# Graph attention in fp32 on one core: the reciprocals of the softmax sums are turned as 32 columns and spread by DMA instead of as 128 columns copied out by ScalarE

## Chip, cores, metric

One core of one Trainium2 chip runs the whole program in one launch. The metric is the device time in microseconds; each kernel is run several times, and the median counts. The host only transposes and permutes arrays before the launch.

## What is computed

32 graphs of 256 nodes and 256 features, 8 heads of 32 features. Cut to what matters:

```python
q, k, v = proj(x, Wq, bq), proj(x, Wk, bk), proj(x, Wv, bv)      # 8 heads of 32
scores  = einsum('bhqd,bhkd->bhqk', q, k) * 32 ** -0.5
attn    = softmax(scores * (adj + adj), axis=-1)
ctx     = einsum('bhqk,bhkd->bhqd', attn, v)
out     = layernorm(x + ctx.reshape(b, 256, 256) @ Wo.T + bo)
```

The kernel works with unnormalised exponentials: it sums each row of `exp(...)`, and multiplies the context by the reciprocal of that sum. The change is about how these reciprocals ("shares": 256 nodes x 8 heads for a graph) get to the layout of the context.

## The kernel before, in words

Engines: TensorE (PE), VectorE (DVE), ScalarE (ACT), GpSimd (POOL), SyncE (SP, which only issues DMAs). Every engine runs its own stream of instructions, in an order that is written out by hand as a loop of steps: `step(g)` for graph g, with eight slots `o` = 0 to 7, one for each head. Waits on semaphores tie the streams together. An instruction never overtakes the one before it on its engine.

Slot o of step g holds, on each engine, among other things:

- **PE**: `turn_probs(g, o)` (four transposes of 128x128, the exponentials of head o, L263), then `rows` (two matmuls, the scores of the head four ahead, L251); further, by slot: at o = 1 `weigh_v(g-1)` (the context of the graph before, 32 matmuls into `ctx_bank`, L337), at o = 2 `turn_shares(g-1)` (L313), at o = 4 `project_v(g+2)` (L307), at o = 7 `project_out(g-1)` (L351), and at o = 0 or 3, 5 and 6 a half of `project_kq` (three matmuls of 512 columns into the one `proj_bank`, L291). The half at o = 5 is the first of a new chunk and waits until ACT has read the chunk before out of `proj_bank` (`kq_out`, L287).
- **DVE**: `reduce_rows` (scores times mask with a running maximum, L415) for the head three ahead, `move_turned(g, o)` (`turn_bank` to SBUF, L430; for o = 0 and 4 ACT does it), `lower_top` (L423); at o = 0 to 3 residual and statistics, at o = 4 `scale_context(g-1)` (L443), at o = 6 `divide(g)` (the reciprocals, L436).
- **ACT**: `exp` (two activations, L542) for the head two ahead, `move_turned` for o = 0 and 4 (L552), at o = 4 (and 7) `read_kq` (`proj_bank` to SBUF, L573), at o = 3 `copy_inverse(g-1)` (L558). In the stream the last of these stands right behind `exp(g, 5)`, and `exp(g, 6)`, `move_turned(g, 4)` and `read_kq` follow it.
- **POOL**: cuts values into a high and a low fp32r part, bias, normalisation, and at o = 7 `spread_shares(g)` (L681).
- **SP**: `fill_stacks` fills the stacks of K and Q of a pair of graphs with 16 DMAs of 256 KB (two per `fill`, L187): eight for K once `cut_kq` number 1 is through, eight for Q once number 3 is; and a load of x. SP works only in odd steps.

The path of the shares before: DVE makes them as 128 partitions x 16 (`shares`); POOL copies each 32 times side by side (`wide`, 128x512); PE turns `wide` with four 128x128 transposes into `inv_bank`; ACT copies `inv_bank` (128x512) to `inverse`; DVE multiplies the context by `inverse`.

```python
319                wait(pe, inverted, g)
320                for half_ in range(2):
321                    for t in range(T):
322                        last = nc.tensor.transpose(inv_bank[:, half_ * S + t * P:half_ * S + (t + 1) * P],
323                                                   wide[:, t, J * half_:J * (half_ + 1), :].rearrange("p h d -> p (h d)"),
324                                                   ident[:])
```

Of the kernel before, what the change touches and what calls it, by code (L numbers as in the profile page):

```python
# [18 lines left out]
P = 128  # L19
B, S, E = 32, 256, 256  # L20
H, D = 8, 32
T = S // P
J = P // D
# [2 lines left out]
LOWEST = -3.4028234e38  # L26
FACTOR = 2.0 * float(D) ** -0.5
RING = 4
TURNED = 12


# [10 lines left out]
def build(nc, x, x_t, adj, adj_t, wq, wk, wv, wo, bq, bk, bv, bo, out):  # L42
    ctx = ExitStack()
    with ctx:
        def sb(name, shape, dt=F32):
            return ctx.enter_context(nc.sbuf_tensor(name, shape, dt))
# [4 lines left out]
        def sem(name):  # L51
            return ctx.enter_context(nc.semaphore(name))
# [13 lines left out]
        top = sb("top", [P, 2, H, T])  # L66
        low_top = sb("low_top", [P, 2, H, T])
        sums = sb("sums", [P, 2, T, H])
        shares = sb("shares", [P, T, H])
        probs = sb("probs", [P, RING, T * S])  # L70
        turned_probs = sb("turned_probs", [P, TURNED, T * S])
        wide = sb("wide", [P, T, H, D])
        inverse = sb("inverse", [P, 2 * S])
        context = sb("context", [P, 2 * S])
        ctx_parts = sb("ctx_parts", [P, 2, 2, 2, S], F32R)
# [5 lines left out]
        ident = sb("ident", [P, P])  # L81
# [26 lines left out]
        rows_made, rows_used, top_ready = sem("rows_made"), sem("rows_used"), sem("top_ready")  # L108
        probs_ready, turned = sem("probs_ready"), sem("turned")
        moved_dve, moved_act = sem("moved_dve"), sem("moved_act")  # L110
        shares_ready, widened, inv_made = sem("shares_ready"), sem("widened"), sem("inv_made")
        ctx_made, inverted, ctx_ready = sem("ctx_made"), sem("inverted"), sem("ctx_ready")
        ctx_high, ctx_low = sem("ctx_high"), sem("ctx_low")
        out_made, y_ready, stats_ready, mean_ready = (
# [9 lines left out]
        def wait(eng, what, value):  # L124

            if value > 0:
                eng.wait_ge(what, value)
# [22 lines left out]
        def is_graph(g):  # L150
            return 0 <= g < B

        def is_pair(g):
            return 0 <= g // 2 < PAIRS
# [37 lines left out]
        @block.sync  # L192
        def _(sp):
            for t in range(T):
                sp.dma_start(xt[:, t, :], x_t[0][:, t * 2 * S:(t + 1) * 2 * S]).then_inc(xt_first[t], 16)
            sp.dma_start(w_whole[:, 1], wq).then_inc(weight_in[1], 16)
            for tile, bias_dram in ((b_k, bk), (b_q, bq)):
                sp.dma_start(tile[:], bias_dram.rearrange("(j d) t -> d j t", j=J)).then_inc(biases_in, 16)
            for n, dram in ((2, wv), (3, wo)):
                sp.dma_start(w_whole[:, n], dram).then_inc(weight_in[n], 16)  # L200
            for tile, dram in ((b_v, bv), (b_o, bo)):
                sp.dma_start(tile[:], dram).then_inc(biases_in, 16)

            def load_x_t(pair):

                sp.wait_ge(xt_low, 2 * pair)
                sp.dma_start(xt[:].rearrange("p t s -> p (t s)"), x_t[pair]).then_inc(xt_in, 16)

            def fill_stacks(pair):
                for which in range(2):  # L210
                    sp.wait_ge(kq_low, 4 * pair + 2 * which + 2)
                    for j in range(J):
                        if pair > 1:

                            sp.wait_ge(rows_made, 8 * (2 * pair - 3) + 2 * j + 2)
                        fill(sp, pair, which, j)

            def step(g):
                if g % 2 == 0:
                    return  # L220
                if is_pair(g + 5):
                    load_x_t((g + 5) // 2)
                if is_pair(g + 3):
                    fill_stacks((g + 3) // 2)

            load_x_t(1)
            for j in range(J):
                fill(sp, 0, 0, j)
            load_x_t(2)

            sp.wait_ge(kq_low, 4)
            for j in range(J // 2, J):
                fill(sp, 0, 1, j)
            fill_stacks(1)
            run_steps(step)

        @block.tensor
        def _(pe):
# [72 lines left out]
                last.then_inc(v_made, 1)  # L311

            def turn_shares(g):  # L313
                pe.wait_ge(widened, g + 1)
                if g == 0:

                    pe.wait_ge(bias_ready, 1)

                wait(pe, inverted, g)
                for half_ in range(2):  # L320
                    for t in range(T):
                        last = nc.tensor.transpose(inv_bank[:, half_ * S + t * P:half_ * S + (t + 1) * P],  # L322
                                                   wide[:, t, J * half_:J * (half_ + 1), :].rearrange("p h d -> p (h d)"),
                                                   ident[:])
                last.then_inc(inv_made, 1)

            def weigh_v(g):
                pe.wait_ge(v_ready, g + 1)
# [52 lines left out]
            def step(g):  # L381
                for o in range(H):
                    if is_graph(g):
                        turn_probs(g, o)
                    if o < 4 and is_graph(g):
                        rows(g, o + 4)
                    if o >= 4 and is_graph(g + 1):
                        rows(g + 1, o - 4)
                    if (g % 2, o) in KQ_SLOTS:
                        ahead = kq_ahead(g, o)  # L390
                        if is_pair(g + ahead):
                            project_kq((g + ahead) // 2, *KQ_SLOTS[g % 2, o])
                    if o == 1 and g == 0:
                        project_v(1)
                    if o == 1 and is_graph(g - 1):
                        weigh_v(g - 1)
                    if o == 2 and is_graph(g - 1):
                        turn_shares(g - 1)
                    if o == 4 and is_graph(g + 2):
                        project_v(g + 2)  # L400
                    if o == 7 and is_graph(g - 1):
                        project_out(g - 1)

            run_steps(step)

        @block.vector
        def _(dve):
# [24 lines left out]
            def divide(g):  # L432
                dve.wait_ge(probs_ready, H * g + H)

                wait(dve, widened, g)
                nc.vector.reciprocal(shares[:], sums[:, g % 2]).then_inc(shares_ready, 1)  # L436

            def scale_context(g):
                dve.wait_ge(ctx_made, g + 1)
                dve.wait_ge(inverted, g + 1)  # L440

                wait(dve, ctx_low, g)
                nc.vector.tensor_tensor(context[:], ctx_bank[:], inverse[:], ALU.mult).then_inc(ctx_ready, 1)  # L443
# [84 lines left out]
        def _(act):  # L528
# [22 lines left out]
                    act.wait_ge(bias_ready, 1)  # L551
                nc.scalar.copy(turned_probs[:, (H * g + o) % TURNED, :], turn_bank[o % 2][:]).then_inc(moved_act, 1)  # L552

            def copy_inverse(g):
                act.wait_ge(inv_made, g + 1)

                wait(act, ctx_ready, g)
                nc.scalar.copy(inverse[:], inv_bank[:]).then_inc(inverted, 1)  # L558

            def cut_x(pair, t):  # L560
                if pair == 0:
# [64 lines left out]
            def step(g):  # L626
                for o in range(H):
                    if o < 6 and is_graph(g):
                        exp(g, o + 2)
                    if o >= 6 and is_graph(g + 1):  # L630
                        exp(g + 1, o - 6)
                    if is_graph(g) and o in ON_ACT:
                        move_turned(g, o)
                    if o == 1 and g % 2 == 0 and is_pair(g + 2):
                        load_masks((g + 2) // 2)
                    if o == 2 and g % 2 == 0 and is_pair(g):
                        load_x(g // 2)
                    if (g % 2, o) in KQ_CUT_SLOTS:
                        ahead = kq_ahead(g, o)
                        if is_pair(g + ahead):  # L640
                            read_kq((g + ahead) // 2, KQ_CUT_SLOTS[g % 2, o])
                    if o == 2 and g == 0:
                        copy_v(1)
                    if o == 3 and is_graph(g - 1):
                        copy_inverse(g - 1)
                    if o == 5 and is_graph(g + 2):
                        copy_v(g + 2)
                    if (g % 2, o) in X_SLOTS and is_pair(g + 4):
                        cut_x((g + 4) // 2, X_SLOTS[g % 2, o])
                    if o == 2 and is_graph(g - 3):  # L650
                        store(g - 3)
# [6 lines left out]
        def _(pool):  # L658
# [13 lines left out]
            def low_x(pair, t):  # L672
                pool.wait_ge(xt_high, 2 * pair + t + 1)
                nc.gpsimd.tensor_tensor(xt_parts[:, pair % 2, 1, t, :], xt[:, t, :], xt_parts[:, pair % 2, 0, t, :].bitcast(F32),  # L674
                                        ALU.subtract).then_inc(xt_low, 1)

            def spread_shares(g):
                pool.wait_ge(shares_ready, g + 1)

                wait(pool, inv_made, g)  # L680
                nc.gpsimd.tensor_copy(wide[:].rearrange("p t h d -> p (t h) d"),  # L681
                                      shares[:].rearrange("p t h -> p (t h)").unsqueeze(2).to_broadcast([P, T * H, D])
                                      ).then_inc(widened, 1)

            def cut_context(g):
                high, low = (ctx_parts[:, g % 2, n].rearrange("p f s -> p (f s)") for n in range(2))
# [47 lines left out]

            def step(g):
                for o in range(H):
                    if o == 7 and is_graph(g):
                        spread_shares(g)
                    if (g % 2, o) in X_SLOTS and is_pair(g + 4):
                        low_x((g + 4) // 2, X_SLOTS[g % 2, o])  # L740
                    if o == 2 and is_graph(g - 1):
# [56 lines left out]
```

## Time and profile before

| | |
|---|---|
| median of 3 runs | 473.74 us (472.96 to 474.92) |
| the profiled execution, its own time | 472.42 us |
| its span, first to last instruction | 470.6 us |
| busy: PE, DVE, ACT, POOL | 446.9, 403.4, 384.3, 345.4 us |
| granted PE clock, mean | 0.988 of full speed |

The sums further on are made against the profiled execution. Busy times of an engine are overlapped with those of the others. A matmul's duration in the timeline reaches from its start to its modelled end, and matmuls overlap, so what a group of matmuls occupies of PE is read from its start to the start of the next group.

### The profile page before, as it was taken

The numbers are of one execution on the slowest core, as the hardware profiler recorded it, in microseconds if no ns is written. First come the engines' busy times: TensorE is split into PE (matmuls) and PEld (weight loads), VectorE is DVE, ScalarE is ACT, GpSimd is POOL, SyncE is SP. The second block draws the span as 40 slices with busy tenths as digits, with TensorE's granted clock in tenths as the row PEclk, the third lists the DMA queues.
The fourth block names the chain that finished last, engine by engine and source line by source line (L and its number), as shares of the span: only waits on it lengthen the run. The fifth ranks groups of instructions, "written<-read, shape, count | busy, mean of one in ns | idle before, by whom it ended". The sixth has DMA issues, their size and how long they took to land.

```text
span 470.6 us, 13017 instructions
## 1 busy us (share of the span) xinstructions
PE 446.9 (95%) x3846; PEld 380.7 (81%) x3846; DVE 403.4 (86%) x1712; ACT 384.3 (82%) x1252; POOL 345.4 (73%) x476
## 2 busy tenths in 40 slices
PE   5889999999999999999999999999999999999962
PEld 4588888988888898888888888888888888888642
DVE  4568889998888898988889988888998888899961
ACT  5488889888888988888899888889988888888840
POOL 0464787869698786968878696878869687865555
PEclk9999999999999999999999999999999999999995
DMA  6986655658666564867656476765647685462211
GB/s 223 353 312 231 242 214 169 251 184 288 247 236 255 169 253 172 286 247 258 234 180 255 183 262 248 272 239 179 252 181 247 247 287 206 158 256 93 70 36 45
DMA packets 37319, 102.57 MB, mean 218 GB/s; under 512 B 5889, under 2 KB 14082, under 8 KB 37250
## 3 DMA queue, kind: packets, MB, share of 16 engines
q1 hardware_dynamic: 23474, 75.26, 43.5%
q10 hardware_dynamic: 13776, 26.48, 16.6%
q8 instruction: 32, 0.52, 0.4%
q14 instruction: 37, 0.30, 0.2%
HBM read 26.22 MB, written 8.39 MB: 74 GB/s over the span
## 4 chain that ended last, share of the span: by engine, by line
PE 84%; DVE 7%; issue 4%; ACT 3%; POOL 2%; DMA 1%; POOLq 0%; DVEq 0%; ACTq 0%
PE turn_bank L263 21%; PE proj_bank L291 18%; PE ctx_bank L337 11%; PE row_bank L251 11%; PE out_bank L351 9%; PE out_bank L307 9%; DVE probs L415 4%; PE inv_bank L322 3%; ACT probs L542 2%; PE row_bank L276 1%; DMA turned_probs<-in_wk 1%; DVE low_top L423 1%; POOL xt_parts L674 1%; DVE stats L455 1%; PE turn_bank L276 1%
## 5 line engine op out<-in xcount | busy, mean ns | idle before, releaser
L542 ACT ACTIVATE probs<-probs,low_top 128x256 f32<-128x256 f32 x512 | 255.7, 503 | 55.9 <-DVE low_top L423 51.8
L415 DVE CUSTOM_DVE_ANT_0 probs<-row_bank,adj_rows 128x256 f32<-128x256 f32 x512 | 192.0, 413 | 7.7 <-PE row_bank L251 5.5
L430 DVE COPY turned_probs<-turn_bank 128x512 f32<-128x512 f32 x192 | 132.3, 689 | 36.7 <-PE turn_bank L263 35.6
L263 PE MATMUL turn_bank<-ident,probs 128*128 128x128 f32 x1024 | 155.3, 274 | 3.1 <-ACT turned_probs L552 1.4
L263 PEld LDWEIGHTS turn_bank<-ident,probs 128*128 128x128 f32 x1024 | 120.9, 140 | 32.8 <-ACT probs L542 16.5
L251 PE MATMUL row_bank<-stack 128*128 128x256 f32 x512 | 123.2, 322 | 2.6 <-issue 1.7
L291 PE MATMUL proj_bank<-xt_parts,w_parts 128*128 128x512 f32 x360 | 105.2, 401 | 1.8 <-ACT whole L573 1.3
L542 ACT ACTIVATION_READ_ACCUMULATOR probs<-probs,low_top 128x1 f32 x512 | 97.7, 191 | 0.0
L251 PEld LDWEIGHTS row_bank<-stack 128*128 128x128 f32 x512 | 77.1, 191 | 5.2 <-issue 4.2
L668 POOL TENSOR_TENSOR parts<-whole,parts 128x512 fp32r<-128x512 f32 x60 | 77.3, 1288 | 5.0
L689 POOL CAST ctx_parts<-context 128x512 fp32r<-128x512 f32 x32 | 19.6, 612 | 73.7 <-DVE context L443 73.7
L291 PEld LDWEIGHTS proj_bank<-xt_parts,w_parts 128*128 128x128 f32 x360 | 59.2, 188 | 11.2 <-issue 1.5
L337 PE MATMUL ctx_bank<-turned_probs,v 128*32 128x256 f32 x1024 | 61.9, 382 | 0.0
L351 PE MATMUL out_bank<-w_parts,ctx_parts 128*128 128x256 f32 x384 | 52.0, 286 | 3.9 <-POOL ctx_parts L691 3.9
L351 PEld LDWEIGHTS out_bank<-w_parts,ctx_parts 128*128 128x128 f32 x384 | 48.7, 193 | 4.4 <-POOL ctx_parts L691 4.4
L307 PE MATMUL out_bank<-w_parts,xt_parts 128*128 128x256 f32 x384 | 51.2, 283 | 0.0
L674 POOL TENSOR_TENSOR xt_parts<-xt,xt_parts 128x512 fp32r<-128x512 f32 x30 | 38.6, 1305 | 15.3 <-ACT xt_parts L567 15.3
L307 PEld LDWEIGHTS out_bank<-w_parts,xt_parts 128*128 128x128 f32 x384 | 48.1, 191 | 0.4 <-issue 0.4
L337 PEld LDWEIGHTS ctx_bank<-turned_probs,v 128*32 128x32 f32 x1024 | 30.0, 109 | 20.9
L691 POOL TENSOR_TENSOR ctx_parts<-context,ctx_parts 128x512 fp32r<-128x512 f32 x32 | 41.3, 1292 | 2.6
L666 POOL CAST parts<-whole 128x512 fp32r<-128x512 f32 x60 | 37.0, 617 | 8.5 <-DMA stack<-parts 5.5
L415 DVE DVE_READ_ACCUMULATOR2_ANT top<- 128x1 f32 x512 | 42.8, 83 | 0.0
(48 smaller groups left out, 462.1 us busy)
## 6 DMA issues: line engine op xcount, KB each, us to landing
stack<-parts SPq DMA_DIRECT2D x252, 256.0 KB, 3.2
adj_rows<-in_adj ACTq DMA_DIRECT2D x16, 512.0 KB, 4.5
xr<-in_x ACTq DMA_DIRECT2D x16, 512.0 KB, 7.2
out<-result ACTq DMA_DIRECT2D x32, 256.0 KB, 4.7
xt<-in_x_t SPq DMA_DIRECT2D x15, 512.0 KB, 5.0
stack<-parts ACTq DMA_DIRECT2D x4, 256.0 KB, 3.8
xt<-in_x_t SPq DMA_DIRECT2D x2, 256.0 KB, 3.6
turned_probs<-in_wk ACTq DMA_DIRECT2D x1, 256.0 KB, 3.7
```

What stands on the lines that cost most here:

```text
L251: last = nc.tensor.matmul(row_bank[o % 2][:, t * S:(t + 1) * S], q[:, t * P:(t + 1) * P], key, start=(t == 0), stop=True, skip_group_check ...
L263: last = nc.tensor.transpose(turn_bank[o % 2][:, c * S + t * P:c * S + (t + 1) * P], probs[:, o % RING, t * S + c * P:t * S + (c + 1) * P] ...
L291: last = nc.tensor.matmul(proj_bank[:], w_parts[:, a, c // 2, t, features], xt_parts[:, pair % 2, b, t, :], start=(half_ == 0 and n == 0), ...
L307: last = nc.tensor.matmul(out_bank[:, tile * E:(tile + 1) * E], xt_parts[:, (n // 2) % 2, a, t, nodes], w_parts[:, c, 2, t, :], start=(til ...
L337: last = nc.tensor.matmul(ctx_bank[c:c + D, half_ * S:(half_ + 1) * S], v[:, (g // 2) % 2, g % 2, t, o * D:(o + 1) * D], turned_probs[:, ( ...
L351: last = nc.tensor.matmul(out_bank[:, n * E:(n + 1) * E], ctx_parts[:, g % 2, a, f, nodes], w_parts[:, b, 3, f, :], start=(n == 0 and i == 0),
L415: last = nc.vector.tensor_tensor_reduce(probs[:, o % RING, t * S:(t + 1) * S], row_bank[o % 2][:, t * S:(t + 1) * S], adj_rows[:, (n // 2) ...
L430: nc.vector.tensor_copy(turned_probs[:, (H * g + o) % TURNED, :], turn_bank[o % 2][:]).then_inc(moved_dve, 1)
L542: last = nc.scalar.activation(tile, tile, ACT.Exp, bias=low_top[:, n % 2, o, t:t + 1], accum_out=sums[:, n % 2, t, o:o + 1])
L668: nc.gpsimd.tensor_tensor(parts[:, 2 * (c // 2) + 1, cut], whole[:, c % 2, :], parts[:, 2 * (c // 2), cut].bitcast(F32), ALU.subtract).the ...
L674: nc.gpsimd.tensor_tensor(xt_parts[:, pair % 2, 1, t, :], xt[:, t, :], xt_parts[:, pair % 2, 0, t, :].bitcast(F32), ALU.subtract).then_inc ...
L691: nc.gpsimd.tensor_tensor(low, context[:], high.bitcast(F32), ALU.subtract).then_inc(ctx_low, 1)
```

## The change

The shares are now made four times side by side (128x64). PE turns 32 columns a tile: two transposes whose stationary side is 128x32 and whose moving side is the 128-column identity, at o = 7 of the same step, behind `project_out`. ACT copies 32 partitions x 256 columns to `share_rows` at o = 0 of the next step. SP then issues two DMAs; each reads 16 partitions of `share_rows` and writes every row to eight partitions of `inverse`. POOL's copy is gone. DVE's multiplication waits for both DMAs. SP's fills for a pair stand in another order: the K fills of a pair, and six of its Q fills, in an even step behind the spread of the shares; the last two Q fills and the load of x in the odd step, behind the spread there.

```diff
-        shares = sb("shares", [P, T, H])
+        shares = sb("shares", [P, T, H * SPREAD])
-        wide = sb("wide", [P, T, H, D])
+        share_rows = sb("share_rows", [H * SPREAD, T * P])
...
+            def spread_shares(g):
+                sp.wait_ge(rows_out, g + 1)
+
+                wait(sp, ctx_ready, g)
+                for half_ in range(2):
+                    rows = J * SPREAD
+                    sp.dma_start(inverse[:, half_ * S:(half_ + 1) * S],
+                                 share_rows[rows * half_:rows * (half_ + 1), :].unsqueeze(1).to_broadcast(
+                                     [rows, D // SPREAD, S])).then_inc(inverted, 16)
 
             def step(g):
+                if is_graph(g - 1):
+                    spread_shares(g - 1)
                 if g % 2 == 0:
-                    return
-                if is_pair(g + 5):
-                    load_x_t((g + 5) // 2)
-                if is_pair(g + 3):
-                    fill_stacks((g + 3) // 2)
+                    if g > 0 and is_pair(g + 2):
+                        fill_stack((g + 2) // 2, 0, range(J))
+                    if is_pair(g + 2):
+                        fill_stack((g + 2) // 2, 1, range(J - 1))
+                else:
+                    if is_pair(g + 1):
+                        fill_stack((g + 1) // 2, 1, [J - 1])
+                    if is_pair(g + 5):
+                        load_x_t((g + 5) // 2)
...
             def turn_shares(g):
-                pe.wait_ge(widened, g + 1)
+                pe.wait_ge(shares_ready, g + 1)
...
-                wait(pe, inverted, g)
-                for half_ in range(2):
-                    for t in range(T):
-                        last = nc.tensor.transpose(inv_bank[:, half_ * S + t * P:half_ * S + (t + 1) * P],
-                                                   wide[:, t, J * half_:J * (half_ + 1), :].rearrange("p h d -> p (h d)"),
-                                                   ident[:])
-                last.then_inc(inv_made, 1)
+                wait(pe, rows_out, g)
+                for t in range(T):
+                    last = nc.tensor.transpose(inv_bank[0:H * SPREAD, t * P:(t + 1) * P], shares[:, t, :], ident[:])
+                last.then_inc(shares_turned, 1)
...
-                    if o == 2 and is_graph(g - 1):
-                        turn_shares(g - 1)
...
+                    if o == 7 and is_graph(g):
+                        turn_shares(g)
...
-                wait(dve, widened, g)
-                nc.vector.reciprocal(shares[:], sums[:, g % 2]).then_inc(shares_ready, 1)
+                wait(dve, shares_turned, g)
+                nc.vector.reciprocal(shares[:].rearrange("p t (h r) -> p (t h) r", r=SPREAD),
+                                     sums[:, g % 2].rearrange("p t h -> p (t h)").unsqueeze(2).to_broadcast(
+                                         [P, T * H, SPREAD])).then_inc(shares_ready, 1)
...
-                dve.wait_ge(inverted, g + 1)
+                dve.wait_ge(inverted, 32 * g + 32)
...
-            def copy_inverse(g):
-                act.wait_ge(inv_made, g + 1)
-
-                wait(act, ctx_ready, g)
-                nc.scalar.copy(inverse[:], inv_bank[:]).then_inc(inverted, 1)
+            def copy_shares(g):
+                act.wait_ge(shares_turned, g + 1)
+
+                wait(act, inverted, 32 * g)
+                nc.scalar.copy(share_rows[:], inv_bank[0:H * SPREAD, 0:T * P]).then_inc(rows_out, 1)
...
+                    if o == 0 and is_graph(g - 1):
+                        copy_shares(g - 1)
...
-                    if o == 3 and is_graph(g - 1):
-                        copy_inverse(g - 1)
...
-            def spread_shares(g):
-                pool.wait_ge(shares_ready, g + 1)
...
```

How the instructions stand on PE, from `project_out` at o = 7 of one step to the slot o = 3 of the next. Before:

```order
L351 MATMUL out_bank<-w_parts,ctx_parts 128x256 x12
L263 MATMUL turn_bank<-ident,probs 128x128 x4
L251 MATMUL row_bank<-stack 128x256 x2
L291 MATMUL proj_bank<-xt_parts,w_parts 128x512 x3
L263 MATMUL turn_bank<-ident,probs 128x128 x4
L251 MATMUL row_bank<-stack 128x256 x2
L337 MATMUL ctx_bank<-turned_probs,v 32x256 x16
L263 MATMUL turn_bank<-ident,probs 128x128 x4
L251 MATMUL row_bank<-stack 128x256 x2
L322 MATMUL inv_bank<-ident,wide 128x128 x4
L263 MATMUL turn_bank<-ident,probs 128x128 x4
L251 MATMUL row_bank<-stack 128x256 x2
```

The same stretch of PE in the changed kernel (its line numbers are its own):

```order
L365 MATMUL out_bank<-w_parts,ctx_parts 128x256 x12
L338 MATMUL inv_bank<-ident,shares 32x128 x2
L280 MATMUL turn_bank<-ident,probs 128x128 x4
L268 MATMUL row_bank<-stack 128x256 x2
L308 MATMUL proj_bank<-xt_parts,w_parts 128x512 x3
L280 MATMUL turn_bank<-ident,probs 128x128 x4
L268 MATMUL row_bank<-stack 128x256 x2
L351 MATMUL ctx_bank<-turned_probs,v 32x256 x16
L280 MATMUL turn_bank<-ident,probs 128x128 x4
L268 MATMUL row_bank<-stack 128x256 x2
L280 MATMUL turn_bank<-ident,probs 128x128 x4
L268 MATMUL row_bank<-stack 128x256 x2
```

The transposes of the shares went from behind the context's matmuls (o = 2) to ahead of them (o = 7 of the step before), and from four to two.

ACT, from the slot o = 0 of an odd step to o = 5, before (`x2` is the exponentials of one head):

```order
L542 ACTIVATE probs,sums<-probs,low_top 128x256 x2
L552 COPY turned_probs<-turn_bank 128x512
L542 ACTIVATE probs,sums<-probs,low_top 128x256 x4
L595 DMA out<-result 128x2x256
L542 ACTIVATE probs,sums<-probs,low_top 128x256 x2
L558 COPY inverse<-inv_bank 128x512
L542 ACTIVATE probs,sums<-probs,low_top 128x256 x2
L552 COPY turned_probs<-turn_bank 128x512
L573 ACTIVATE whole<-proj_bank,b_k 128x512
```

and in the changed kernel:

```order
L558 ACTIVATE probs,sums<-probs,low_top 128x256 x2
L574 COPY share_rows<-inv_bank 32x256
L568 COPY turned_probs<-turn_bank 128x512
L558 ACTIVATE probs,sums<-probs,low_top 128x256 x4
L611 DMA out<-result 128x2x256
L558 ACTIVATE probs,sums<-probs,low_top 128x256 x4
L568 COPY turned_probs<-turn_bank 128x512
L589 ACTIVATE whole<-proj_bank,b_k 128x512
```

The copy that stood between the exponentials of heads 5 and 6 is gone from there; the smaller one stands at o = 0.

SP's queue in the changed kernel, with its waits, from the third to sixth Q fill of an even step over the odd step to the head of the next even one:

```order
L189 DMA stack<-parts 64x1x1024 [waits rows_made]
L189 DMA stack<-parts 64x1x1024
L189 DMA stack<-parts 64x1x1024 [waits rows_made]
L189 DMA stack<-parts 64x1x1024
L225 DMA inverse<-share_rows 128x1x256 [waits ctx_ready,rows_out]
L225 DMA inverse<-share_rows 128x1x256
L189 DMA stack<-parts 64x1x1024 [waits rows_made,kq_low]
L189 DMA stack<-parts 64x1x1024
L209 DMA xt<-in_x_t 128x1024 [waits xt_low]
L225 DMA inverse<-share_rows 128x1x256 [waits ctx_ready,rows_out]
L225 DMA inverse<-share_rows 128x1x256
L189 DMA stack<-parts 64x1x1024 [waits rows_made,kq_low]
```

Between the spreads of an even and an odd step stand eight K fills and six Q fills; the spread of the odd step is queued behind those six, where the seventh and eighth Q fill stood before.

## Rows read from the trace of the kernel before

**Rows 1.** The page: span, and the engines' busy times.

```profile
span 470.6 us, 13017 instructions
...
PE 446.9 (95%) x3846; PEld 380.7 (81%) x3846; DVE 403.4 (86%) x1712; ACT 384.3 (82%) x1252; POOL 345.4 (73%) x476
```

**Rows 2.** The chain in order of time: `weigh_v` of graphs 1 and 27.

```profile
53.06 1.86 PE ctx_bank L337 x32
...
408.12 1.86 PE ctx_bank L337 x32
```

**Rows 3.** Timeline of PE, an even step: start us, us, engine, line, operation.

```profile
246.02 0.66 PE L263 MATMUL turn_bank<-ident,probs 128*128 128x128 f32 x4
...
246.76 0.60 PE L322 MATMUL inv_bank<-ident,wide 128*128 128x128 f32 x4
247.19 0.60 PE L263 MATMUL turn_bank<-ident,probs 128*128 128x128 f32 x4
...
251.02 0.48 PE L251 MATMUL row_bank<-stack 128*128 128x256 f32 x2
251.48 0.93 PE L291 MATMUL proj_bank<-xt_parts,w_parts 128*128 128x512 f32 x3
252.25 0.60 PE L263 MATMUL turn_bank<-ident,probs 128*128 128x128 f32 x4
252.60 0.48 PE L251 MATMUL row_bank<-stack 128*128 128x256 f32 x2
252.93 0.85 PE L291 MATMUL proj_bank<-xt_parts,w_parts 128*128 128x512 f32 x3
253.62 0.60 PE L263 MATMUL turn_bank<-ident,probs 128*128 128x128 f32 x4
```

**Rows 4.** Timeline of DVE, same step; in brackets idle time and who ended it.

```profile
244.03 0.69 DVE L430 COPY turned_probs<-turn_bank 128x512 f32<-128x512 f32 x1 [0.24 <-PE turn_bank L263]
...
246.72 0.69 DVE L430 COPY turned_probs<-turn_bank 128x512 f32<-128x512 f32 x1 [0.93 <-PE turn_bank L263]
...
248.40 0.69 DVE L430 COPY turned_probs<-turn_bank 128x512 f32<-128x512 f32 x1
249.00 0.14 DVE L423 TENSOR_REDUCE low_top<-top 128x2 f32<-128x2 f32 x1
```

**Rows 5.** Timeline of ACT, same step.

```profile
247.51 0.51 ACT L542 ACTIVATE probs<-probs,low_top 128x256 f32<-128x256 f32 x1 [1.09 <-DVE low_top L423]
...
248.51 0.57 ACT L558 COPY inverse<-inv_bank 128x512 f32<-128x512 f32 x1
249.18 0.51 ACT L542 ACTIVATE probs<-probs,low_top 128x256 f32<-128x256 f32 x1
...
250.18 0.56 ACT L552 COPY turned_probs<-turn_bank 128x512 f32<-128x512 f32 x1
250.65 0.69 ACT L573 ACTIVATE whole<-proj_bank,b_q 128x512 f32<-128x512 f32 x1
```

**Rows 6.** Groups by line and shape: busy us, mean ns of one.

```profile
L436 DVE RECIPROCAL shares<-sums 128x16 f32<-128x16 f32 x32 | 7.8, 244 | 0.0
L461 DVE BATCH_NORM_AGGREGATE mean_var<-stats 128x2 f32<-128x6 f32 x64 | 7.6, 161 | 0.1
```

**Rows 7.** SP's fills at 258.0 to 259.4 us: issue ns min/median/max, and landing.

```profile
L187 SPq DMA_DIRECT2D stack<-parts x3: 615/760/1320, 258.0 to 259.4; - x3
...
DMA to landing us min/median/max: 3.2/3.6/3.7
```

**Rows 8.** Timeline of the end: context, share transposes' copy, multiplication of graph 31.

```profile
454.42 1.93 PE L337 MATMUL ctx_bank<-turned_probs,v 128*32 128x256 f32 x32
...
456.98 0.59 ACT L558 COPY inverse<-inv_bank 128x512 f32<-128x512 f32 x1 [5.30 <-PE inv_bank L322]
457.65 0.69 DVE L443 TENSOR_TENSOR context<-ctx_bank,inverse 128x512 f32<-128x512 f32 x1 [1.36 <-issue]
```

**Rows 9.** Timeline of DVE, the odd step behind it: its multiplication of the context.

```profile
263.80 0.69 DVE L443 TENSOR_TENSOR context<-ctx_bank,inverse 128x512 f32<-128x512 f32 x1
```

More of the change, by code:

```diff
@@ L28 @@
 RING = 4
+SPREAD = 4
 TURNED = 12
@@ L110, in build @@
         moved_dve, moved_act = sem("moved_dve"), sem("moved_act")
-        shares_ready, widened, inv_made = sem("shares_ready"), sem("widened"), sem("inv_made")
+        shares_ready, shares_turned, rows_out = sem("shares_ready"), sem("shares_turned"), sem("rows_out")
         ctx_made, inverted, ctx_ready = sem("ctx_made"), sem("inverted"), sem("ctx_ready")
@@ L207, in load_x_t, with fill_stack @@
                 sp.dma_start(xt[:].rearrange("p t s -> p (t s)"), x_t[pair]).then_inc(xt_in, 16)
[L209 to L216, printed above, removed]
+            def fill_stack(pair, which, heads):
+                sp.wait_ge(kq_low, 4 * pair + 2 * which + 2)
+                for j in heads:
+                    if pair > 1:
+                        sp.wait_ge(rows_made, 8 * (2 * pair - 3) + 2 * j + 2)
+                    fill(sp, pair, which, j)
+            def spread_shares(g):
[6 more added lines that the diff above has]
+                                     [rows, D // SPREAD, S])).then_inc(inverted, 16)
             def step(g):
+                if is_graph(g - 1):
+                    spread_shares(g - 1)
                 if g % 2 == 0:
-                    return
-                if is_pair(g + 5):
-                    load_x_t((g + 5) // 2)
-                if is_pair(g + 3):
-                    fill_stacks((g + 3) // 2)
+                    if g > 0 and is_pair(g + 2):
[7 more added lines that the diff above has]
+                        load_x_t((g + 5) // 2)
             load_x_t(1)
@@ L233, in _ @@
                 fill(sp, 0, 1, j)
-            fill_stacks(1)
+            fill_stack(1, 0, range(J))
             run_steps(step)
@@ L675, in low_x @@
                                         ALU.subtract).then_inc(xt_low, 1)
-            def spread_shares(g):
-                pool.wait_ge(shares_ready, g + 1)
[L680 to L683, printed above, removed]
             def cut_context(g):
@@ L736, in step @@
                 for o in range(H):
-                    if o == 7 and is_graph(g):
-                        spread_shares(g)
                     if (g % 2, o) in X_SLOTS and is_pair(g + 4):
```

## Prediction

> **What bounds the kernel now.** I read four views in this order. The page first: PE is busy for 446.9 of 470.6 us, more than any other engine [rows 1]. That suggests that whatever PE is spared is won, and two transposes fewer per graph would be a gain. The chain in order of time gives the beat: from `weigh_v` of graph 1 to that of graph 27 are 355.06 us, 13.66 us a graph, even and regular [rows 2].
>
> Then the timeline of PE, because a busy share of nearly 100% doesn't tell whether PE waits: a matmul's bar reaches to its modelled end and hides a short wait. Starts do tell. At o = 6 the first `proj_bank` matmul starts 0.33 us after the two `row_bank` matmuls, and the next transposes 0.69 us after that. At o = 5 the same two distances are 0.46 and 0.77 us [rows 3]. So PE loses 0.13 + 0.08 = 0.21 us at o = 5 of this step, although the profile calls it busy. What it waits for is `kq_out`: ACT's read of `proj_bank` begins at 250.65 and takes 0.69, to 251.34 [rows 5], and the matmul begins at 251.48, where the earlier beat of 0.33 would have had it at 251.35.
>
> Last, the way back from that read, in DVE's and ACT's timelines. ACT: read at 250.65, ahead of it the copy of turned head 4 at 250.18, ahead of that the exponentials of head 6 from 249.18, without a gap [rows 5]. These begin when DVE's `lower_top` ends, 249.00 + 0.14 = 249.14 [rows 4]; the share copy on ACT had ended at 248.51 + 0.57 = 249.08 and didn't hold them. DVE works without idle time from 246.72 on, and at 246.72 it had waited 0.93 us for PE: for `turn_probs(g, 2)`, which starts at 246.02 [rows 3, 4]. So a chain **turn(g, 2) on PE, then DVE, then ACT, then the `proj_bank` matmul at o = 5** takes 251.48 - 246.02 = 5.46 us. PE's own work between these two points is 5.46 - 0.21 = 5.25 us. In every step PE is held there by this chain, if only by 0.2 us; from o = 5 to the next o = 2 PE is the bound itself.
>
> **The change, part by part.**
>
> *Transposes taken out at o = 2.* Four of them occupy PE from 246.76 to 247.19: 0.43 us, 0.1075 each [rows 3]. They lie inside the window from turn(g, 2) to o = 5. PE's own work there falls to 5.25 - 0.43 = 4.82 us, but the window stays 5.46 us, since none of its links on DVE and ACT is touched. Worth: 0. What is late next is the same thing as before; PE's wait at o = 5 only grows, from 0.21 to 0.64 us.
>
> *Two transposes put in at o = 7.* They stand behind `project_out`, in the part of the step in which PE is the bound. The moving side is the identity with its 128 columns as before; only the stationary side is narrower. Nearest row for one: 0.1075 us [rows 3], so 0.215 us a graph. Bounds: half of that if the narrow stationary side sets the pace (I know no row that gives it, so the lower end is the half), 0.30 us, if the two take half of the 0.60 us of the bar of four and nothing overlaps. I take 0.215, by the row of the same operation with the same moving side. That is 31 x 0.215 = 6.7 us over graphs 0 to 30; graph 31 is in the end, below.
>
> *Reciprocals, 64 instead of 16 columns.* 244 ns for 16 columns, 161 ns for the small operation on 6 [rows 6]: 8.3 ns a column, so 48 more cost 0.40 us (ends: 0.05 us, if columns cost next to nothing, and 0.73 us, four times the whole). The Trainium skill (VectorE: DVE Perf Modes, the part on the ALU slices) says that the reciprocal is an iterative divide with a repeat count of 8; at the page's clock of 0.96 GHz that would be an estimated 48 x 8 / 0.96 = 0.40 us, and the row agrees. On the path: nothing. DVE idles 0.24 us and 0.93 us waiting for PE at o = 1 and 2 of the next step [rows 4], 1.17 in all, after the reciprocal and before the chain above begins. Without that cover it would be 32 x 0.40 = 13 us.
>
> *ACT.* The copy of 0.57 us leaves o = 3, ahead of which and behind which ACT waits for DVE (1.09 us idle at 247.51, and the begin at 249.18 by `lower_top`) [rows 5]: worth at most 249.18 - 249.14 = 0.04 us. The smaller copy comes in at o = 0, at most 0.57 us; the 1.09 us of idle time behind it hide that. *POOL's* copy off: POOL is busy for 345 us [rows 1] and releases nothing in the chain: 0.
>
> *SP.* The two spread DMAs come between fills. In an even step they are first in the queue once the rows are out. In an odd one they queue behind six Q fills and take the place of the seventh and eighth; the fills there took 0.6 to 1.3 us to issue and at most 3.7 us to land; the seventh began between 258.0 and 259.4, at some 258.7 [rows 7]. With a second issue of up to 1.3 us the spread lands at 262.5 to 263.7. DVE multiplies at 263.80 [rows 9]. It fits: 0. K fills come some 3 us later in the even step, and are not used before o = 4 of the odd one: 0.
>
> *The end.* For graph 31 the multiplication now starts at 457.65, 3.23 us after `weigh_v` begins at 454.42 [rows 8]. Changed: two transposes from about 454.4 (0.4 us to their end), ACT's copy (0.4), two issues (0.6 each) of which the second lands 2 to 3.2 us after its start. That gives 457.9 to 459.0, I take 458.35: +0.7 us.
>
> Sum: 472.42 + 6.7 + 0.7 = 479.8 us for the profiled execution. The median before is 1.3 us above that execution, so the forecast for the median is **481.1 us**, slower by 1.6%. About 0.5% (2.4 us, 471.4 to 476.1) is what a measurement of this kernel can tell from no change.
>
> **Rivals.**
>
> *Faster: PE's work is the bound after all.* If the 0.21 us at o = 5 is no wait but the cost of changing operations, PE gains 4 transposes and pays 2, -0.215 us in 31 graphs: 473.7 - 6.7 + 0.7 = 467.7 us. For it: the page's 95%, and the idle column, which shows no wait at o = 5. Against: o = 6 has the same change of operations without the 0.21 us, and ACT's read ends 0.14 us ahead of the start. It decides if the chain can shrink by 0.43 us. 12%.
>
> *No change: the chain shrinks by half of that.* With the share copy off ACT, the exponentials of head 6 or the read could come 0.2 us earlier, and window and o = 7 cancel: 473.7 + 0.7 = 474.4 us. Against it stand the 0.04 us above. It would also come about if DVE ran faster without POOL's copy beside it. 13%.
>
> *Slower by less: narrow transposes cost half.* 31 x 0.11 + 0.7 = +4.1: 477.8 us. 10%.
>
> *Much slower: the spread lands late in odd steps.* DVE would wait with the multiplication, and `reduce_rows` and `move_turned` behind it in its queue. The 1.17 us that DVE idles in a step [rows 4] are the room; beyond it PE would wait too. At 1 us beyond, 16 odd steps give 16 us more: 497 us. For it: the source is 16 neighbouring partitions, and six fills are ahead. Against: 0.1 to 1.3 us of room, then DVE's. The Trainium skill (SBUF — State Buffer, Door 1: The DMA port swizzle) says that partitions 0 to 15 reach 4 of 16 ports, some 109 GB/s; an estimate from that is 1.2 us for the 128 KB of one DMA. By it the spread would land about 1 us later than a fill, at the edge of the room, and no row here shows a DMA with such a source. 5%.
>
> **How the numbers follow.** Forecast 60%, narrow transposes 10%, late spread 5%: slower 0.75. No change 0.13, faster 0.12. The forecast's own range is 478.5 to 485: 0.30 us a pair gives +2.6, the reciprocals' cover gone in the last four steps +1.6, the end +0.7 or less. The range to hold 8 in 10 leaves out the faster rival and the late spread (17%) and reaches down to no change: 473.5 to 485.5.
>
> **What would show it.** Right: the beat between two `weigh_v` is 13.87 us instead of 13.66; PE's start at o = 5 still follows the end of ACT's read by 0.05 to 0.15 us, and the idle column now shows that wait; turn(g, 2) to o = 5 still takes 5.4 to 5.5 us; `inv_bank` matmuls lie 0.11 us apart; the reciprocal takes 0.64 us; DVE's multiplication never waits for a DMA except for graph 31. Wrong: a window clearly under 5.4 us (then the faster rival), a DVE wait for the spread at o = 4 of odd steps (then the late one), or `inv_bank` starts 0.05 us apart.

## The result, and the profile after

| | before | changed |
|---|---|---|
| median | 473.36 us (472.96 to 474.92, 4 runs) | 483.61 us (482.58 to 484.82, 4 runs) |
| profiled execution, its span | 472.42, 470.6 us | 484.82, 482.1 us |
| busy PE, DVE, ACT, POOL | 446.9, 403.4, 384.3, 345.4 us | 447.2, 412.1, 377.7, 326.3 us |

The ratio is 1.0213, 95% interval 1.0187 to 1.0239: slower by 2.1%. Forecast were 481.1 us and a range of 473.5 to 485.5.

The page of the changed kernel:

```profile
span 482.1 us, 12935 instructions
...
PE 447.2 (93%) x3782; PEld 374.7 (78%) x3782; DVE 412.1 (85%) x1712; ACT 377.7 (78%) x1252; POOL 326.3 (68%) x444
```

PE lost 64 matmuls and its busy time still rose by 0.3 us against [rows 1]. That column can't show the gain or the loss: a bar runs to its modelled end.

The beat, by the chain in order of time (start, us, what): `weigh_v` of graphs 1 and 27, which answer to [rows 2].

```profile
53.03 1.86 PE ctx_bank L351 x32
...
413.14 1.86 PE ctx_bank L351 x32
```

360.11 us for 26 steps, 13.85 us a step, 0.19 more than before. That is 5.05 of the 11.5 us by which the span grew. The timeline of PE in an odd step, from turn(g, 2) on (start us, us, engine, line, operation; idle time before in brackets), shows the window that [rows 3] have for an even one:

```profile
262.61 0.66 PE L280 MATMUL turn_bank<-ident,probs 128*128 128x128 f32 x4
...
264.71 0.60 PE L280 MATMUL turn_bank<-ident,probs 128*128 128x128 f32 x4
265.21 0.47 PE L268 MATMUL row_bank<-stack 128*128 128x256 f32 x2
...
266.95 0.60 PE L280 MATMUL turn_bank<-ident,probs 128*128 128x128 f32 x4
267.30 0.48 PE L268 MATMUL row_bank<-stack 128*128 128x256 f32 x2
267.97 0.96 PE L308 MATMUL proj_bank<-xt_parts,w_parts 128*128 128x512 f32 x3 [0.18 <-ACT whole L589]
268.77 0.60 PE L280 MATMUL turn_bank<-ident,probs 128*128 128x128 f32 x4
...
270.81 1.57 PE L365 MATMUL out_bank<-w_parts,ctx_parts 128*128 128x256 f32 x12
272.21 0.38 PE L338 MATMUL inv_bank<-ident,shares 128*32 128x128 f32 x2
272.43 0.60 PE L280 MATMUL turn_bank<-ident,probs 128*128 128x128 f32 x4
```

From 262.61 to 267.97 are 5.36 us (the even step behind it: 5.45), the lengths of before (5.36 in odd steps, 5.46 in even ones), although 0.43 us of work are gone from the window. PE now waits longer at two places. At o = 5 the distance from the `row_bank` matmuls to the `proj_bank` matmul went from 0.36 to 0.67 us in odd steps and from 0.46 to 0.76 in even ones, and now the idle column names the releaser: ACT's read. At o = 4 the scores start 0.50 us behind the transposes (264.71 to 265.21), where the kernel before has 0.35; the experiments come back to this. Together that is 0.45 us, about what was taken out. The two new transposes sit at 272.21 and take 0.22 us.

ACT, same step, answers to [rows 5]:

```profile
265.76 0.51 ACT L558 ACTIVATE probs<-probs,low_top 128x256 f32<-128x256 f32 x1 [0.58 <-DVE low_top L437]
...
266.77 0.56 ACT L568 COPY turned_probs<-turn_bank 128x512 f32<-128x512 f32 x1
267.23 0.68 ACT L589 ACTIVATE whole<-proj_bank,b_k 128x512 f32<-128x512 f32 x1
```

Where the share copy stood, ACT idles 0.58 us and starts head 6 when DVE lets it, as before. The read ends at 267.91, PE starts at 267.97.

The groups that the change touched (busy us, mean ns of one), against [rows 6]:

```profile
L450 DVE RECIPROCAL shares<-sums 128x64 f32<-128x64 f32 x32 | 17.3, 541 | 0.0
L338 PE MATMUL inv_bank<-ident,shares 128*32 128x128 f32 x64 | 12.2, 272 | 0.0
L574 ACT COPY share_rows<-inv_bank 32x256 f32<-32x256 f32 x32 | 11.1, 347 | 3.1 <-PE inv_bank L338 3.1
```

The other half of the loss lies in the last steps. Timeline of PE, `weigh_v` of graphs 27 to 30, before:

```profile
408.05 1.93 PE L337 MATMUL ctx_bank<-turned_probs,v 128*32 128x256 f32 x32
420.01 1.93 PE L337 MATMUL ctx_bank<-turned_probs,v 128*32 128x256 f32 x32
432.03 1.93 PE L337 MATMUL ctx_bank<-turned_probs,v 128*32 128x256 f32 x32
444.04 1.93 PE L337 MATMUL ctx_bank<-turned_probs,v 128*32 128x256 f32 x32
```

and changed, graphs 27 to 31:

```profile
413.07 1.93 PE L351 MATMUL ctx_bank<-turned_probs,v 128*32 128x256 f32 x32
425.32 1.93 PE L351 MATMUL ctx_bank<-turned_probs,v 128*32 128x256 f32 x32
440.99 1.93 PE L351 MATMUL ctx_bank<-turned_probs,v 128*32 128x256 f32 x32
453.25 1.93 PE L351 MATMUL ctx_bank<-turned_probs,v 128*32 128x256 f32 x32
463.85 1.93 PE L351 MATMUL ctx_bank<-turned_probs,v 128*32 128x256 f32 x32
```

One step takes 15.67 instead of 12.02 us. DVE's and PE's timelines in it:

```profile
433.60 0.69 DVE L459 TENSOR_TENSOR context<-ctx_bank,inverse 128x512 f32<-128x512 f32 x1 [2.23 <-DMA inverse<-share_rows]
```

```profile
435.12 0.47 PE L268 MATMUL row_bank<-stack 128*128 128x256 f32 x2 [2.26 <-DVE top L429]
```

DVE stands 2.23 us at its multiplication, since the spread lands late; PE's scores stand behind DVE. This is the late-spread rival, in one step of the tail. SP's queue shows why there:

```profile
411.82 1.22 SPq L225 DMA_DIRECT2D inverse<-share_rows  x2
413.14 14.92 SPq L189 DMA_DIRECT2D stack<-parts  x14
428.16 1.63 SPq L225 DMA_DIRECT2D inverse<-share_rows  x2
```

The eight K fills and six Q fills between two spreads take SP 14.92 us without a gap. Behind a full even step the same queue just fits: the spread at 400.39 begins 1.1 us behind its `weigh_v`. But the projections of K and Q are gone from the even step here, which takes 12.25 us instead of 13.88, so the spread behind it begins at 428.16, 2.84 us behind the `weigh_v` of 425.32.

The wait isn't all of the 3.65 us. PE had run no matmul for 2.26 us, and behind that its granted clock was 0.50 of full speed (1.2 instead of 2.4 GHz; the columns behind the us are busy times, PE's clock, DMA share, GB/s):

```profile
435.75:438.75 3.00, 3.00 (x15) 3.00 (x16) 3.00 (x14) 2.11 (x8) 2.55 (x7) 0.50 0.02 5
```

From the transposes at 435.73 to the `inv_bank` transposes at 439.33 are 3.60 us; in another execution of this kernel, in which PE stood for 1.40 us and the clock stayed full, they are 2.40. So where the late step is 3.35 us longer than a clean one of this kernel (12.32 us, further on), some 2.2 are waiting and 1.2 slower matmuls.

At the end the multiplication of graph 31 comes 5.33 us after its `weigh_v` begins, where [rows 8] have 3.23:

```profile
463.95 0.36 ACT L574 COPY share_rows<-inv_bank 32x256 f32<-32x256 f32 x1 [3.07 <-PE inv_bank L338]
464.34 1.19 SPq L225 DMA_DIRECT2D inverse<-share_rows  x2
464.83 0.38 ACTq L611 DMA_DIRECT2D out<-result  x1
...
469.18 0.69 DVE L459 TENSOR_TENSOR context<-ctx_bank,inverse 128x512 f32<-128x512 f32 x1 [3.69 <-issue]
```

The account of the span: 26 full steps +5.05, the late step +3.65, the three other steps of the tail +0.76, the end +2.10, the rest under 0.1; together 11.5 us.

### The profile page after: what moved, and what is told of

Read it like the earlier page. It is cut to its first block, busy times and chain, and to the rows that moved or that the text cites. A ratio compares the mean times of both kernels' runs of the same rounds, so it can differ in the third digit from the quotient of the medians.

```text
span 482.1 us, 12935 instructions
## 1 busy us (share of the span) xinstructions
PE 447.2 (93%) x3782; PEld 374.7 (78%) x3782; DVE 412.1 (85%) x1712; ACT 377.7 (78%) x1252; POOL 326.3 (68%) x444
## 4 chain that ended last, share of the span: by engine, by line
PE 59%; DVE 13%; ACT 12%; issue 10%; POOL 3%; DMA 2%; SPq 1%; DVEq 0%; POOLq 0%; ACTq 0%
PE proj_bank L308 14%; PE turn_bank L280 14%; PE ctx_bank L351 12%; PE out_bank L365 9%; PE row_bank L268 6%; DVE probs L429 5%; ACT probs L558 5%; ACT whole L589 3%; ACT turned_probs L568 3%; DVE stats L471 2%; DVE turned_probs L444 2%; DVE low_top L437 2%; PE inv_bank L338 1%; PE row_bank L293 1%; DMA inverse<-share_rows 1%
## 5 line engine op out<-in xcount | busy, mean ns | idle before, releaser
L429 DVE DVE_READ_ACCUMULATOR2_ANT top<- 128x1 f32 x512 | 41.8, 82 | 0.0
```

The costliest lines, as they stand in the source:

```text
L429: last = nc.vector.tensor_tensor_reduce(probs[:, o % RING, t * S:(t + 1) * S], row_bank[o % 2][:, t * S:(t + 1) * S], adj_rows[:, (n // 2) ...
```

## Experiments

Two theories stood against each other. The **chain theory**: PE is held once a step at o = 5 by the way turn(g, 2), DVE, ACT, so work taken out between o = 2 and o = 5 gains nothing, and work put in at o = 7 costs its full time. The **work theory**: PE's own work is the bound, and the loss comes from the DMAs, the longer reciprocals or late transfers.

### Less work in the window: nothing gained

```diff
-                for half_ in range(2):
-                    for t in range(T):
+                for half_ in range(2 if g == 0 else 1):
+                    for t in range(T if g == 0 else 1):
```

> The kernel before, with three of the four share transposes at o = 2 left out after graph 0 (so most of `inverse` is stale). Chain theory (the way from turn(g, 2) over DVE and ACT to the proj_bank matmul at o = 5 holds PE): 0.32 us less work of PE in that window, the window stays 5.36 to 5.46 us, the beat 13.62 to 13.69 us, time 473.4 within 1.5 us. Rival (PE's work is the bound): 31 x 0.32 = 10 us less, 463.4 us.

Measured: 473.40 us against 473.77, ratio 0.9991 (0.9967 to 1.0014). Graphs 1 to 27 by the chain in order of time:

```profile
55.96 1.86 PE ctx_bank L337 x32
...
410.91 1.86 PE ctx_bank L337 x32
```

354.95 us, 13.65 a step, as before. The window has the lengths of before too, and PE's distance at o = 5 grew to 0.75 and 0.66 us from 0.46 and 0.36: what PE was spared it waits. The 10 us of the work theory are excluded, and with them the faster rival.

### Two transposes more at o = 7 of the kernel before

```diff
                     if o == 7 and is_graph(g - 1):
                         project_out(g - 1)
+                    if o == 7 and is_graph(g) and g > 0:
+                        pe.wait_ge(inverted, g)
+                        for t in range(T):
+                            nc.tensor.transpose(inv_bank[:, t * P:(t + 1) * P], ident[:], ident[:])
```

> The kernel before, with two more 128x128 transposes of the identity at o = 7 behind project_out; everything else as before, no DMA for the shares. Theory that the place at o = 7 is the cost: +0.218 us a graph, 31 graphs, 473.4 + 6.8 = 480.2 us, beat 13.84 to 13.91. Rival (the slowdown of the change is the DMAs' or the reciprocals', and PE's place costs nothing): 473.4 us.

Measured: 479.37 us, ratio 1.011 (1.008 to 1.014), +5.6 us; the beat was 13.83 to 13.91 us. The place alone costs about what the changed kernel loses in its full steps, without a spread DMA and with the short reciprocal.

### The changed kernel's two transposes done twice

```diff
-                for t in range(T):
+                for t in (*range(T), *range(T)):
```

> The changed kernel, with its two narrow transposes done twice (four at o = 7). Theory: each costs 0.109 us at that place, 32 graphs, 483.6 + 7.0 = 490.6 us, beat 14.04 to 14.10. Rival (the narrow ones cost half, or lie in the cover of something): 483.6 to 487 us.

Measured: 491.29 us, 7.7 more; beat 14.05 and 14.11 us. Here four of them:

```profile
234.51 0.60 PE L338 MATMUL inv_bank<-ident,shares 128*32 128x128 f32 x4
```

The second pair cost 5.83 us over 26 steps, 0.112 us for each transpose. A stationary side of 32 columns instead of 128 doesn't make it cheaper at this place. That settles the narrow rival. The late step of the tail is there too, 15.82 us, with a wait of 1.86 for the spread and a lowered clock behind it.

### The chain cut short: ACT's read first

On both kernels the read of `proj_bank` at o = 4 goes ahead of the copy of turned head 4:

```diff
-                    if is_graph(g) and o in ON_ACT:
+                    if is_graph(g) and o in ON_ACT and o != 4:
                         move_turned(g, o)
...
                             read_kq((g + ahead) // 2, KQ_CUT_SLOTS[g % 2, o])
+                    if is_graph(g) and o == 4:
+                        move_turned(g, o)
```

> The kernel before, with ACT's read of proj_bank at o = 4 ahead of its copy of turned head 4. Chain theory: the chain gets 0.47 us shorter, PE loses its wait of 0.15 to 0.21 us at o = 5 and is then the bound: beat 13.45 to 13.50, 27 steps, 473.4 - 5 = 468.5 us. Rival (the 0.2 us at o = 5 are no wait): 473.4 us or a little more, since turned head 4 comes later.

Measured, on the kernel before: **468.58 us**, ratio 0.9882 (0.9853 to 0.9911). The timeline of PE:

```profile
208.78 0.48 PE L251 MATMUL row_bank<-stack 128*128 128x256 f32 x2
209.11 0.86 PE L291 MATMUL proj_bank<-xt_parts,w_parts 128*128 128x512 f32 x3
209.80 0.60 PE L263 MATMUL turn_bank<-ident,probs 128*128 128x128 f32 x4
```

0.33 and 0.69 us at o = 5, the values of o = 6: the wait is gone, the window is 5.32 us and the beat 13.49 in every step.

> The changed kernel, with ACT's read of proj_bank at o = 4 ahead of its copy of turned head 4. Chain theory: PE waits 0.6 us a step at o = 5; the chain gets 0.47 us shorter, so the beat falls from 13.85 to 13.4 us: 27 x 0.45 = 12 us, 471.5 us. If the next link (scores of the graph ahead at o = 4 waiting for DVE) comes in, part of it: 475. Rival (PE has no such wait): 483.6 us.

Measured, on the changed kernel: 476.14 us, from 472.28 to 478.51 over ten runs. The beat is 13.36 to 13.41 us in most steps, as forecast, and the window 5.01 us. The gain is 7.5 us and not 12. The shorter beat brings the late spread into full steps:

```profile
its engine sat idle before it (us, times) until:
  DMA inverse<-share_rows: 9.2, 16
```

(DVE's waits before its multiplication.) Single steps rise to 14.0 and 14.2 us. This trace is of an execution of 472.84 us, one of the shortest; what the longer ones lost was not traced.

### Fewer fills ahead of the spread

```diff
-                        fill_stack((g + 2) // 2, 1, range(J - 1))
+                        fill_stack((g + 2) // 2, 1, range(J - 2))
...
-                        fill_stack((g + 1) // 2, 1, [J - 1])
+                        fill_stack((g + 1) // 2, 1, [J - 2, J - 1])
```

> The changed kernel, with four Q fills instead of six ahead of the odd step's spread, and four behind it. Theory that the late step of the tail (12.0 to 15.67 us) is a spread queued behind six fills: its two DMAs are issued 1.3 us earlier, the wait of 2.23 us falls to about 0.9 us, 483.6 - 1.5 = 482 us. Rival (it is late for another reason): 483.6 us.

Measured on the changed kernel: 482.75 us, ratio 1.0208 (1.0172 to 1.0243). The tail steps are 12.26, 12.32 and 12.32 us, so the late step is gone from the trace; the medians differ by 0.9 us, no more than their spread.

> The changed kernel with both edits of the two before it: the read of proj_bank first, and four Q fills ahead of the spread. If they are independent: 471.5 - 1.5 = 470 us, 3 us under the kernel before. The shorter beat brings DVE's multiplication no closer to the spread, since both hang on the same turn; if it does, waits for the spread in odd steps show and the time is over 473.

Measured: 470.47 us, ratio 0.9944 (0.9922 to 0.9966), as forecast. DVE's wait for the spread fell from 9.2 us in 16 steps to 0.5 us in one.

To settle the late step, the changed kernel ran again beside one that has two Q fills (`[0]`) ahead of the spread and six (`range(1, J)`) behind it:

> The changed kernel once more, on the chip of the run beside it: 483.6 us. If the late step of the tail comes in every execution, its trace shows one step of 15 us or more between two weigh_v again.

> The changed kernel with two Q fills ahead of the odd spread and six behind it. Late step in every execution: 3.4 us less than the run beside it, no step over 12.4 us in the tail. Late step only in some executions, or the time goes elsewhere: less than 1.5 us between the two medians.

Measured: 484.68 us (ratio 1.022, 1.0187 to 1.0253) and 482.44 us (1.0182, 1.0147 to 1.0218). DVE's multiplication of the late step in the first:

```profile
435.33 0.69 DVE L459 TENSOR_TENSOR context<-ctx_bank,inverse 128x512 f32<-128x512 f32 x1 [1.37 <-DMA inverse<-share_rows]
```

That step took 13.73 us this time, where it was 15.67 before; with one pair of fills ahead it took 12.32. The forecast of 15 us or more was missed, and the 2.2 us between the medians lie between the two values forecast (3.4, and under 1.5), with overlapping intervals. So both traces of the changed kernel have the late step, with a length of its own each time, 1.4 and 3.4 us over a clean one: 1.37 us of waiting alone here, and 2.23 with the lowered clock behind it there. Its mean cost isn't settled closer than that.

### The read still earlier, looking for a version that beats both

On the changed kernel with four Q fills ahead, ACT's read goes ahead of the exponentials of head 6, where ACT idles since the share copy left:

```diff
                 for o in range(H):
+                    if o == 4 and is_pair(g + kq_ahead(g, o)):
+                        read_kq((g + kq_ahead(g, o)) // 2, KQ_CUT_SLOTS[g % 2, o])
                     if o < 6 and is_graph(g):
                         exp(g, o + 2)
```

> The changed kernel with four Q fills ahead of the odd spread, and ACT's read of proj_bank at o = 4 ahead of the exponentials of head 6, in the place that the share copy left free. Chain theory: from turn(g, 2) to o = 5 the window falls from 5.01 us to PE's own work, some 4.85 us, the beat from 13.38 to 13.2: 470.5 - 4.5 = 466 us, under the kernel before and under the kernel before with the read first (468.6). Rival: the exponentials of head 6 come later and hold the transposes of head 6, so the window stays at 5.0 and the time at 470.5.

Measured: 468.76 us, ratio 0.990 (0.9872 to 0.9929). The window stayed at 5.01 us, but neither for the theory's reason nor for the rival's:

```profile
219.72 0.60 PE L280 MATMUL turn_bank<-ident,probs 128*128 128x128 f32 x4
220.23 0.47 PE L268 MATMUL row_bank<-stack 128*128 128x256 f32 x2
220.54 1.59 PE L324 MATMUL out_bank<-w_parts,xt_parts 128*128 128x256 f32 x12
```

```profile
218.32 0.69 DVE L444 COPY turned_probs<-turn_bank 128x512 f32<-128x512 f32 x1 [0.93 <-PE turn_bank L280]
...
219.66 0.42 DVE L429 CUSTOM_DVE_ANT_0 probs<-row_bank,adj_rows 128x256 f32<-128x256 f32 x1
220.00 0.08 DVE L429 DVE_READ_ACCUMULATOR2_ANT top<- 128x1 f32 x1
```

The scores at o = 4 begin 0.51 us after the transposes ahead of them, 0.15 later than at other slots: they wait for a bank that DVE lets go at 220.08. This link was there before the edit: the same distance is 0.50 us in the changed kernel, and 0.50 in the run with the read first and four fills ahead, whose window is 5.01 us as well. So once ACT's read comes first, it is the shorter way from turn(g, 2) over DVE alone to the scores at o = 4 that holds PE, and a still earlier read has nothing to gain in the window.

> The same with two Q fills ahead of the odd spread and six behind it. Theory: what is left of late spreads (one step of 12.85 us in the tail instead of 12.3) goes: 0.5 us less than the run before it, 465.5 us. Rival: the later Q fills now come late for the scores of the next pair, and PE waits for them: over 468 us.

Measured: 470.41 us (five runs from 468.46 to 471.10, and one execution of 730 us at a mean granted clock of 0.559, which no trace here shows), ratio 0.9922 (0.9895 to 0.9949). The tail is clean (12.26, 12.32, 12.32 us), yet no gain shows in the medians; the trace shows no wait of PE for a fill, so the rival's reason isn't seen either.

Best of all runs, by ratio, is the kernel before with the read first, 0.9882; the changed kernel with the read early is within its interval at 0.990.

## Why the prediction was right, point by point

- **The window stays.** Forecast 5.4 to 5.5 us, measured 5.36 and 5.45 us. The prediction put all of PE's longer wait at o = 5 (0.64 us); 0.15 of it lie at o = 4, behind DVE, which it didn't name. PE's own work in the window before was 5.32 us by the run with the read first, not 5.25. Worth of the four transposes at o = 2: 0, and leaving three out of the kernel before gave nothing either.
- **Two transposes at o = 7.** Forecast 0.215 us a step, measured 0.19 (26 steps, 5.05 us). The pair itself costs 0.22; the 0.03 us between the two I didn't follow up. In the 30 steps other than the late one the change cost 5.8 us, where the sum had 6.4.
- **Reciprocals.** Forecast 640 ns, measured 541: 0.30 us more, not 0.40. The slope between two different operations was too steep; 297 ns for 48 columns are 6.2 ns a column. So the estimate from the repeat count of 8 at 0.96 GHz (the Trainium skill, VectorE: DVE Perf Modes, First, the fixed hardware budget), 8.3 ns a column, is above this measurement. In full steps they cost nothing that shows, as forecast: the beat grew by less than the pair of transposes takes. In the tail the clean steps grew by 0.31 us (12.01 to 12.32), with two transposes more and the short reciprocal by 0.14 (12.15). The longer reciprocal would fit the difference; no run changed it alone.
- **ACT, POOL, K fills:** 0, as forecast, as far as the beat shows it; POOL's busy time fell by 19 us.
- **The spread in odd steps** fits in full steps of the changed kernel but for two waits, 0.24 and 0.80 us. Even so, the sign that the prediction had named for the late-spread rival, a DVE wait for the spread in odd steps, did show, in three of them. The room was small, as the shorter beat showed. What failed is the tail: the sum took the late spread as all or nothing over 16 odd steps and put 5% on it. It came in one odd step, behind an even step that is shorter than the fourteen fills queued in it, and cost 3.65 us in the profiled execution and 1.7 in another.
- **The end.** Forecast +0.7 us, measured +2.1. The mis-sized term is the landing: I took 2 to 3.2 us from the issue of the second DMA. It was issued near 464.9 and DVE began at 469.18, 4.2 us later, with a store of results issued between the two. The way up to that issue was 0.3 us shorter than forecast (1.1 us from `weigh_v` instead of 1.4).
- **The sum.** 7.4 us were forecast for the change. Of the profiled execution's 11.5 us of span, the late step (3.65 instead of 0.2) and the end (2.1 instead of 0.7) are 4.8 us more than forecast, the other steps 0.6 less. The medians differ by 10.25 us. The mechanism was right; that the median came within the range is in part luck, since the range's upper end had been made for a dearer pair of transposes and for uncovered reciprocals, not for a late spread.

From the port rule (the Trainium skill, SBUF — State Buffer, Door 1: The DMA port swizzle) the prediction had an estimate of 1.2 us for a spread DMA's 128 KB, and of a landing about 1 us behind a fill's. The 64 spread DMAs landed in 3.9 us in the median, the fills of the same kernel, with 256 KB, in 3.8: 0.1 us apart, but with half the bytes. That is in line with a narrow source, but also with smaller packets; no run here changed the source alone.

## What to carry to other kernels

A busy share of 95% doesn't say that an engine is the bound at every point of a step. Compare the distances of starts for the same operations in two slots. Here the scores, the projection and the next transposes start 1.02 us apart in all at o = 6, and 1.23 (even steps) or 1.16 us (odd ones) at o = 5; a chain over other engines ended there. Work taken out of the window ahead of it gained nothing, while work put behind it cost nearly all of its time. Look for such a chain first (here one swap of two instructions on ACT cut it, 1.2%), then for work to take out, and expect the next link behind it, which held the changed kernel's window at 5.01 us.

A transfer put into a queue that has room in a full step has to be checked in the last steps too, where the rest of the step is shorter and the queue isn't.

## What was not expected of the hardware

A transpose with a 32-column stationary side costs PE 0.11 us, the same as one with 128 columns, although its weight load is recorded as 96 instead of 141 ns. Executions also differ outside the steps. In the run with the transposes left out, which is the kernel before up to graph 0, the first `weigh_v` began at 42.4 us and not at 39.5. PE had stood without a matmul for 2.19 us at 21.4 to 23.6, where it stood for 1.23 us in the trace of before, and behind that its granted clock was 0.50 up to 27.3 us:

```profile
24.00:27.00 3.00, 3.00 (x10) 2.31 (x10) 1.77 (x10) 0.00 (x0) 1.58 (x2) 0.50 0.35 141
```

In the trace of before the clock is full there. From graph 1 on the steps were the same; near the end the clock was 0.50 once more, from 454 to 457.6 us, and the last step took 11.16 instead of 10.38 us. The executions of the kernel before go by this: those with a mean granted clock of 0.983 took 473.8 to 475.8 us, those with 0.987 or 0.988 471.9 to 473.7, the few between lie between. So two single executions can lie 2 to 3 us apart with the same steps. Why PE stood longer at the start in one of them, the profile doesn't name.
